# Lookups in seven pieces and four early turnings in one run, in a DLRM tower on one core

## The reference

```python
e = jnp.stack([tbl_0[ids[:, 0]], ..., tbl_31[ids[:, 31]]], axis=1)   # [2048, 32, 256]
z = jnp.einsum('bnd,bmd->bnm', e, e)[:, iu, ju]                     # pairs i < j: [2048, 496]
h = jnp.concatenate([z, dense_ctx], axis=1)                         # [2048, 512]
h = jnp.maximum(h @ W_top1 + b_top1, 0.0)                           # [2048, 512]
h = jnp.maximum(h @ W_top2 + b_top2, 0.0)                           # [2048, 256]
y = h @ W_top3                                                      # [2048, 1]
```

## Time and profile before

| | us |
|---|---|
| median of three runs | 548.25 (546.71 to 550.8) |
| profiled execution, time | 548.03 |
| its span, first to last instruction | 546.2 |
| TensorE busy | 503.2 (92%) |
| GpSimd busy | 390.7 (72%) |
| VectorE busy | 250.8 (46%) |
| ScalarE busy | 184.0 (34%) |
| TensorE's mean granted clock | 0.994 of full speed |

### The profile page before, as it was taken

The page is one execution under the profiler, slowest core; times in us unless marked ns, Lnnn a source line. Parts: engine busy times, 40 slices in busy tenths (PEclk is TensorE's granted clock), DMA queues, the critical chain, the costliest instruction groups (busy, mean ns, idle before and its releaser), DMA issues.

```text
span 546.2 us, 27461 instructions
## 1 busy us (share of the span) xinstructions
PE 503.2 (92%) x11015; PEld 464.7 (85%) x11015; DVE 250.8 (46%) x592; ACT 184.0 (34%) x355; POOL 390.7 (72%) x418
## 2 busy tenths in 40 slices
PE   0765899999899999999999999999999999999997
PEld 0764799999789899998998989898899988888996
DVE  3665563543536244363625436362543536244142
ACT  1777151421505133050514215050521505142152
POOL 6777767777777777777777777777777777777710
PEclk9998999999999999999999999999999999999999
DMA  8999634444444444444444444454444444443310
GB/s 194 253 254 282 196 101 117 132 119 122 127 122 130 122 122 119 129 116 121 130 123 121 131 123 119 118 131 120 119 131 122 121 124 122 117 115 108 109 32 2
DMA packets 39173, 71.19 MB, mean 130 GB/s; under 512 B 11302, under 2 KB 25382, under 8 KB 39046
## 3 DMA queue, kind: packets, MB, share of 16 engines
q0 software_dynamic: 19728, 53.90, 35.2%
q1 hardware_dynamic: 18550, 15.14, 11.4%
q10 hardware_dynamic: 768, 0.39, 0.3%
HBM read 69.39 MB, written 0.01 MB: 127 GB/s over the span
## 4 chain that ended last, share of the span: by engine, by line
PE 60%; POOL 18%; issue 9%; DMA 7%; DVE 3%; ACT 1%; SPq 1%; DVEq 0%
PE look_ps L395 22%; POOL rows L347 18%; PE quad_ps L417 13%; PE top_ps L476 7%; PE quad_ps L379 6%; PE turn_ps L379 6%; DMA landed<-in_tbl 4%; PE top_ps L497 4%; DMA rows<-in_tbl,row_ids 2%; PE quad_ps L438 1%; DMA ids_across<-in_small_ids 1%; DVE turned L725 1%; PE top_ps L461 1%; DVE one_hot L797 1%; DVE small L787 1%
## 5 line engine op out<-in xcount | busy, mean ns | idle before, releaser
L347 POOL DMA_INDIRECT rows<-in_tbl,row_ids x411 | 390.0, 949 | 129.1 <-issue 114.1
L395 PE MATMUL look_ps<-one_hot,small 125*128 125x256 f32 (+1 forms) x1536 | 220.8, 293 | 8.6 <-DVE small L787 8.5
L395 PEld LDWEIGHTS look_ps<-one_hot,small 125*128 125x128 f32 x1536 | 195.0, 193 | 12.4 <-issue 9.9
L797 DVE TENSOR_SCALAR one_hot<-ids_across,sub_row 125x256 fp32r<-125x256 int32 (+1 forms) x384 | 118.2, 378 | 121.4 <-PE look_ps L395 112.4
L417 PE MATMUL quad_ps<-turned 128*32 128x31 f32 x7680 | 105.0, 199 | 3.5 <-issue 2.2
L417 PEld LDWEIGHTS quad_ps<-turned 128*32 128x32 f32 x7680 | 86.6, 110 | 23.8 <-issue 5.0
L570 ACT ACTIVATE ahead<-look_ps 128x512 f32<-128x512 f32 (+1 forms) x48 | 28.0, 584 | 203.5 <-PE look_ps L395 203.4
L379 PE MATMUL turn_ps<-ident,rows 128*128 128x128 f32 x418 | 62.9, 281 | 20.2 <-DMA rows<-in_tbl,row_ids 16.3
L379 PEld LDWEIGHTS turn_ps<-ident,rows 128*128 128x128 f32 x418 | 46.7, 142 | 24.8 <-issue 17.8
L379 PE MATMUL quad_ps<-ident,rows 128*128 128x128 f32 x404 | 61.1, 280 | 6.5 <-DMA rows<-in_tbl,row_ids 4.3
L561 ACT ACTIVATE turned<-turn_ps 128x512 f32<-128x512 f32 x57 | 36.1, 633 | 60.7 <-PE quad_ps L417 44.8
(11 more groups left out here) (68 smaller groups left out, 199.3 us busy)
## 6 DMA issues: line engine op xcount, KB each, us to landing
area<-in_tbl SPq DMA_DIRECT2D x640, 1.0 KB
rows<-in_tbl,row_ids POOLq DMA_INDIRECT x411
area<-in_tbl ACTq DMA_DIRECT2D x384, 1.0 KB
ids_across<-in_small_ids SPq DMA_DIRECT2D x45, 128.0 KB
landed<-in_tbl SPq DMA_DIRECT2D x6, 896.0 KB
w_sb<-in_W_top SPq DMA_DIRECT2D x4, 256.0 KB
landed<-in_tbl SPq DMA_DIRECT2D x6, 104.0 KB
w_sb<-in_W_top SPq DMA_DIRECT2D x1, 512.0 KB
```

The costliest lines, as they stand in the source:

```text
L347: pool.indirect_dma_start(out=rows[:, n % PLACES, j, :], out_offset=None, in_=tables[f], in_offset=bass.IndirectOffsetOnAxis(ap=row_ids[:, ...
L395: last = pe.matmul(look_ps[:, c * width:(c + 1) * width], small[:, f, r, part, c * P:(c + 1) * P], one_hot[n % 2][:, r, 0:width], start=(r ...
L797: last = dve.tensor_scalar(one_hot[n % 2][:, r, 0:width], ids_across[0:SP, n % IDS_RING, 0:width], sub_row[:, r:r + 1], None, ALU.is_equal)
```

## The change

Three things are changed, all in TensorE's order but one.

1. For tiles 1 to 15 the lookups are cut into seven pieces in place of nine. They stand ahead of portions 1 to 6 and behind portion 7; none stands ahead of portions 0 and 7. With three lookups of 32 products the pieces are 10, 11, 11, 16, 16, 16 and 16 products long.
2. The four early turnings, which stood one each behind portions 3 to 6, stand in one run behind portion 6. Tile 0 keeps its own places for them.
3. In tile 0 the two lookups start later: the fifth lookup stands whole ahead of portion 4, and the sixth in four pieces ahead of portions 5, 6 and 7 and behind portion 7, so portions 0 to 3 come first. On SyncE's queue the sixth list of ids is loaded ahead of the weights in place of behind them.

```diff
-    EARLY_AFTER = [3, 4, 5, 6]
+    EARLY = 4
+    LOOK_AHEAD_OF = [1, 2, 3, 4, 5, 6, 8]
+    EARLY_AFTER = 6
     FIRST_EARLY_AFTER = [0, 1, 2, 3]
...
             for i in range(2, SMALL):
                 load_table(i)
+            load_ids(5)
             sp.dma_start(act_list_sb[:, :], act_list).then_inc(act_list_in, 16)
...
                 sp.dma_start(w1_sb[:, c, :], w1[c * P:(c + 1) * P, :]).then_inc(weights_in, 16)
-            load_ids(5)
...
-                for i in range(len(EARLY_AFTER), BEGIN[t + 1] - BEGIN[t]):
+                for i in range(EARLY, BEGIN[t + 1] - BEGIN[t]):
...
+            def first_look(k):
+
+                fifth, sixth = FIRST[0], FIRST[0] + 1
+                if k == PARTS // 2:
+                    look_up(fifth, 0, PRODUCTS)
+                if k > PARTS // 2:
+                    at = k - PARTS // 2 - 1
+                    look_up(sixth, PRODUCTS * at // (PARTS // 2), PRODUCTS * (at + 1) // (PARTS // 2))
+
             def look_between(t, k):
 
                 made = FIRST[t + 1] - FIRST[t]
+                if k not in LOOK_AHEAD_OF:
+                    return
+                piece, pieces = LOOK_AHEAD_OF.index(k), len(LOOK_AHEAD_OF)
                 for n in range(made):
-                    begin, end = (n * (PARTS + 1) + made - 1) // made, ((n + 1) * (PARTS + 1) + made - 1) // made
-                    if begin <= k < end:
-                        look_up(FIRST[t] + n, PRODUCTS * (k - begin) // (end - begin),
-                                PRODUCTS * (k + 1 - begin) // (end - begin))
+                    begin, end = (n * pieces + made - 1) // made, ((n + 1) * pieces + made - 1) // made
+                    if begin <= piece < end:
+                        look_up(FIRST[t] + n, PRODUCTS * (piece - begin) // (end - begin),
+                                PRODUCTS * (piece + 1 - begin) // (end - begin))
...
                 for k in range(PARTS):
-                    look_between(t, k)
+                    if t > 0:
+                        look_between(t, k)
+                    else:
+                        first_look(k)
...
-                    early_after = EARLY_AFTER if t > 0 else FIRST_EARLY_AFTER
-                    if k in early_after and t + 1 < TILES:
-                        turn(BEGIN[t + 1] + early_after.index(k))
-                look_between(t, PARTS)
+                    if t == 0 and k in FIRST_EARLY_AFTER:
+                        turn(BEGIN[1] + FIRST_EARLY_AFTER.index(k))
+                    if t > 0 and k == EARLY_AFTER and t + 1 < TILES:
+                        for i in range(EARLY):
+                            turn(BEGIN[t + 1] + i)
+                if t > 0:
+                    look_between(t, PARTS)
+                else:
+                    first_look(PARTS)
```

## The result

| | before, us | after, us |
|---|---|---|
| median | 547.60 (546.71 to 550.8, 4 runs) | 605.32 (599.67 to 610.15, 4 runs) |
| ratio | | 1.098, interval 1.0903 to 1.1057 |
| profiled execution, span | 546.2 | 607.1 |
| TensorE's mean granted clock in it | 0.994 | 0.955 |

The change makes the kernel 10% slower. Slower was forecast, with 583 us and a range to 605. The ratio leaves out executions more than 1.5% above the fastest of their kernel, here those of 608.86 and 610.15 us, so it stands for some 602 us, inside the range and 19 us above the forecast; the median of all four lies 0.3 us above the range. The executions of the changed kernel differ mainly by how far the clock fell in them (599.67 us at a mean granted clock of 0.977, 604.24 at 0.966, 608.86 at 0.955).

The account below looks back on a forecast made before the run. TensorE and GpSimd were both taken as full, tied through nine places. Unit 12 of tile 3 at 142.7, twelve tiles 416.9, tile 14 -1.2, the end 23.0: span 581.4, time 583 us, range 565 to 605.

Parts of the forecast that it names:

- the loop: GpSimd waits for unit 0's place, TensorE for rows gathered behind it: 35.5 us a tile, 34.2 with seven gathers.
- The 5.62 us of tile 9: Time between unit 0's turning at 316.07 us and GpSimd's gather of unit 9 into its place at 321.69 us.
- the loop as summed: Main case: GpSimd and TensorE wait for each other every tile, clock up; 575 to 592 us, chance 0.68.
- the rival with the clock down: TensorE's clock falls in the new waits, layer 1 costs 2.4 us more: 612 us, or 595 wide tiles alone; chance 0.14.
- layer 1 to unit 0 turned: TensorE's way from layer 1's start through portion 6 to unit 0's turning: 22.5 + 0.66 = 23.16 us a tile.
- unit 12 of tile 3 turned at: Turning of tile 3's last unit on TensorE, where the sum starts: 142.7 us, as before within 0.3 us.
- landing of unit 12: From the end of the eight gathers on GpSimd to unit 12's turning on TensorE: 300.67 - 298.81 = 1.86 us.
- My waits lie between, nearer the short one: TensorE's waits at units 11 and 12, some 1.5 and 2 us, lie between 6.29 (clock fell) and 1.92 (stayed).
- what is late next: Unit 0's place comes free after 23.16 us, GpSimd wants it after 20.52: GpSimd waits 2.64 us in every tile.
- Layer 2's wait: Behind portion 0, TensorE waits for ScalarE's hidden activations, as no piece covers them: 0.8 us of new wait.
- the change moves none of SyncE's work there: SyncE's row fetches for tile 3's unit 12 stay put, so tile 0's gain, at most 2.97 us, is gone.
- What was to show it: Marks in the changed kernel's profile: unit 9's gather idle near 2.6 + 0.3 us, layer 1 to layer 1 34 to 36 us.

Follow-up runs that it names:

- the last experiment: Kernel before with tile 0's new order and seven pieces, ahead of portions 0 to 4 and 6 and behind 7, early turnings one each: 552.35 us, ratio 1.0037.

## Why the prediction was right, and where it was not

*What bounds the kernel, and the loop: right.* The slack of a place, read unit by unit, was what the kernel lived on. The 5.62 us of tile 9 is the largest: tiles 2 to 15 had 3.1 to 5.6 us, so most tiles had less to spare. With the run behind portion 6 the gather of unit 9 follows unit 0's turning by 0.27 us in all tiles from 2 to 15. Undoing the run, moving it forward or adding a place each gives back about four fifths of the loss or more. The measured time lies in the range, but not by the sum: the loop as summed, with a chance of 0.68, was to give 575 to 592 us. That the range held is owed to the room that it left towards the rival with the clock down.

*The terms of the loop that held.* Eight gathers took 9.71 us (9.70 predicted), seven 8.45. With the clock up, layer 1 to unit 0 turned took 23.38, 23.82 and 22.70 us in tiles 3, 9 and 12 (23.16). From unit 12 of the last tile to the end it took 607.05 - 584.03 = 23.02 us (23.0).

*The terms that were mis-sized.* The profiled span is 607.1 - 581.4 = 25.7 us over the sum:

| term | predicted, us | profiled, us | difference |
|---|---|---|---|
| unit 12 of tile 3 turned at | 142.7 | 145.95 | +3.2 |
| layer 1 to unit 0 turned, tiles 3 to 14, together | 276.7 | 289.7 | +13.0 |
| landing of unit 12, tiles 4 to 15, together | 22.3 | 29.5 | +7.1 |
| unit 12's turning to layer 1, twelve times | 6.0 | 8.1 | +2.1 |

The rest, 0.3 us, is rounding.

The largest is the clock. "My waits lie between, nearer the short one, so the sum has no such cost" is the step that failed. The waits were sized about rightly in their sum (1.5 and 2 us predicted; 2.28 and 0.73 us in tile 8), but the clock fell behind them in eight of the ten tiles 4 to 13. Layer 1 then took 4.4 to 6.0 us from its start to the next portion's, in place of 3.67, which adds up to 13.0 us: as much as the second row. The rival with a chance of 0.14 happened, between its two forms: in eight of the twelve tiles, not in all and not in the wide ones alone, at 1.6 us a tile where it occurred (2.4 estimated), since the clock came back before layer 1 was over. The last row is the same cause: a turning at the low clock, 0.9 us. The Trainium skill ("TensorE: Matmul & The Clock Gate", "Why this matters for your kernels") warns of idle gaps between bursts of matmuls; the idle products, which filled them and made the kernel 12 us faster, agree.

The landing is the second. It was taken from one turning, 1.86 us after its gather, in a tile in which the id list went out at 300.04 us, 1.2 us behind the end of that gather. In the changed kernel the list goes out ahead of that end, and the prediction did not follow this ("what is late next" stopped at GpSimd). The wide tiles kept 1.8 to 2.0 us. Tiles 5 and 10 had 4.40 and 4.05; with the list late they had 2.71 and 3.04. Tiles 6, 9 and 12 had 2.4 to 2.7 us, but there TensorE did not wait for unit 12: it came late from unit 11, which had landed after 3.0 to 3.3 us. With the list late, unit 12 had 1.80 and 1.84 in tiles 6 and 12, and 2.48 in tile 9. For what is left in tiles 5, 9 and 10 no cause was shown. SyncE's queue in that tile of the kernel before:

```profile
300.04 0.42 SPq L276 DMA_DIRECT2D ids_across<-in_small_ids  x1
```

*Layer 2's wait:* 0.8 us predicted, 0.29 to 0.54 measured. The end of the wait was right: where the clock is up, layer 2 starts 4.97 us after layer 1 began (3.49 + 0.69 + 0.8 = 4.98 predicted). TensorE only comes to it later, since layer 1 takes 3.67 us to a portion that stands right behind it, and the portion more than 0.69. In tile 9 of the changed kernel, where layer 1 began at 368.30 us:

```profile
371.97 0.92 PE L419 MATMUL quad_ps<-turned 128*32 128x31 f32 x64
373.27 1.99 PE L499 MATMUL top_ps<-w_sb,area 128*128 128x256 f32 x8 [0.39 <-ACT area L652]
```

A wait that was not foreseen came beside it: the features, 0.30 us a tile, which stand behind the last piece, now 16 products long in place of 10 or 11. With a last piece of 11, in the last experiment, it is gone.

*Tile 0:* "the change moves none of SyncE's work there" is wrong. SyncE's fetches stand behind the lists for the one-hot matrices, so they follow the tiles; with tile 0 earlier they went out earlier, at 131.16 us in the changed kernel and 132.53 in the kernel with tile 0's order alone, against 134.50. The gain is real (0.4%). In the changed kernel the loop, which closes in tile 2 already with a slow layer 1 there (5.14 us), took it: hence 145.95 and not 142.7.

*What was to show it.* Unit 9's gather ended by a turning, once a tile: yes, with 3.2 to 8.3 us idle in tiles 3 to 14 where 2.9 was said; of the 4.5 us in tiles 8 and 9, 1.0 and 1.6 are layer 1 at the low clock in the tile before. TensorE's waits for rows: once or twice a tile and 2.4 to 4.4 us together in tiles 3 to 13, where two or three times and some 4 us were said. GpSimd's idle time: 62 us more, where 30 was said. TensorE's busy time from tile 3 on: 393.75 us, 22 more, where 5 was allowed: this mark failed, and 13.0 us of it are layer 1 at the low clock. Layer 1 to layer 1: 36.9 us in the mean of tiles 3 to 13, where 34 to 36 was said.

## What to carry over

Where two full engines share a ring of buffers, read for one unit how long its place has been free before the other engine asks for it: that slack, not a busy share, says how far a releasing instruction may be moved back. Once the slack is gone, every term of the way round counts in full, each tile, so price also what the new waits do to the clock and which other queue's transfers now fall into them. Merging small pieces saves their overhead, but takes away what covered another engine's hand-over and what stood between runs of short matmuls; here that cost as much as it saved or more.

## What the runs showed of the hardware

- Two waits around one short turning brought the clock down in this kernel more surely than a single wait about as long as the two together. In the changed kernel it fell in all six tiles with two waits (1.21 and 1.96 us in tile 13, 2.28 and 0.73 in tile 8), and after the single waits of 4.38 and 3.92 us in tiles 5 and 10. Of the single waits of 2.36 to 2.66 us one in four brought it down; in tile 9, 2.61 us left it at 1.00. It is no fixed matter of the waits' length: with the late list, 1.15 and 1.81 us in tile 4 left it up, and 1.17 and 1.81 in tile 13 brought it down.

TensorE in tile 9 of the changed kernel, and the stretch around it:

```profile
367.37 0.77 PE L381 MATMUL quad_ps<-ident,rows 128*128 128x128 f32 x5 [2.61 <-DMA rows<-in_tbl,row_ids]
...
368.30 3.74 PE L478 MATMUL top_ps<-area,w_sb 128*128 128x128 f32 x32
```

```profile
363.00:372.00 9.00, 6.39 (x61) 6.04 (x59) 5.81 (x12) 4.08 (x7) 6.72 (x8) 1.00 0.46 119
```

- Two gram portions with nothing between hold TensorE 2.01 us, where one alone holds it 0.69 us or 0.94 (the one at 325.37 above). What limits them was not tried.
- The rows of unit 12 landed 1.8 to 2.0 us after its last gather in the changed kernel's wide tiles, and 4.40 us after it in tile 5, where a 128-KB list went out 1.9 us ahead of the gather's end (2.71 with the list late). Unit 11 landed after 3.0 to 3.3 us in six tiles of the changed kernel, and after 1.8 to 1.9 in five of these six with the list late.
